# Three row-sum DMAs per item issued from ScalarE's queue instead of SyncE's, in a fused cross-attention and FFN kernel

## The reference, cut to what matters

```python
q, k, v = Wq @ ln(x), Wk @ ctx, Wv @ ctx
x1 = x + Wskip @ ln(x) + softmax(q.T @ k / sqrt(128)) applied to v   # 1024 x 256 scores
w  = (unpack_nibbles(qweight) - round(zeros / scales)) * scales        # 1024 x 1024
y  = x1 + ln(x1) @ w + bias
```

## Time and profile before

| | us |
|---|---|
| three runs | 566.91, 565.77, 566.85 (median 566.85) |
| the profiled execution | 567.06 |
| its span, first to last instruction | 565.2 |
| TensorE busy (matmuls) | 511.2 (90% of the span) |
| VectorE busy | 440.3 (78%) |
| GpSimd busy | 426.3 (75%) |
| ScalarE busy | 376.0 (67%) |

### The profile page before, as it was taken

One profiled execution on the slowest core, in us unless ns is written; L12 is line 12 of the kernel. 1 busy time (PEld: TensorE's weight loads), 2 busy tenths in 40 slices (PEclk: granted clock), 3 DMA queues, 4 the chain that ended last, 5 costly groups with the idle time before them and its releaser, 6 DMA issues.

```text
span 565.2 us, 9260 instructions
## 1 busy us (share of the span) xinstructions
PE 511.2 (90%) x2700; PEld 314.5 (56%) x2700; DVE 440.3 (78%) x1009; ACT 376.0 (67%) x844; POOL 426.3 (75%) x619
## 2 busy tenths in 40 slices
PE   2167789999999999999999999999999999999976
PEld 2054455656665665555566666555656665565532
DVE  2967778888988788888988878888898888886631
ACT  2277767776677677677677777767667776776510
POOL 1252778889888888888988888887988888888653
PEclk9996999999999999999999999999999999999989
DMA  8023678779778878888888988887888798866652
GB/s 316 29 66 66 130 160 184 175 174 191 172 165 160 169 180 187 183 176 182 168 185 164 163 175 182 178 189 169 184 172 174 177 146 183 195 122 147 139 118 92
DMA packets 236787, 91.65 MB, mean 162 GB/s; under 512 B 219200, under 2 KB 223808, under 8 KB 236736
## 3 DMA queue, kind: packets, MB, share of 16 engines
q1 hardware_dynamic: 236016, 90.92, 75.0%
q10 hardware_dynamic: 720, 0.14, 0.1%
HBM read 23.87 MB, written 16.78 MB: 72 GB/s over the span
## 4 chain that ended last, share of the span: by engine, by line
PE 48%; DVE 20%; SPq 10%; DMA 7%; ACT 6%; issue 5%; POOL 3%; POOLq 0%; ACTq 0%
PE ps_y L730 27%; PE ps_e L691 7%; DMA sb_xnt_lo<-sb_xn_lo 6%; PE ps_o L714 5%; SPq L173 4%; SPq L179 4%; PE ps_o L710 3%; SPq L165 3%; DVE sb_x L500 3%; DVE sb_st L434 3%; DVE sb_neg_max L481 2%; DVE sb_p_lo L490 2%; DVE sb_st L505 2%; ACT sb_p_hi L358 2%; PE ps_kv L699 2%
## 5 line engine op out<-in xcount | busy, mean ns | idle before, releaser
L730 PE MATMUL ps_y<-sb_wf,sb_xnt_hi 128*128 128x512 f16 x512 | 195.8, 382 | 13.7 <-DMA sb_xnt_lo<-sb_xn_lo 13.5
L730 PE MATMUL ps_y<-sb_wf,sb_xnt_lo 128*128 128x512 f16 x512 | 195.1, 381 | 0.0
L349 ACT ACTIVATE sb_prob<-ps_e,sb_neg_max 128x256 f32<-128x256 f32 x256 | 118.3, 471 | 62.5 <-DVE sb_neg_max L481 62.4
L235 POOL TENSOR_SCALAR sb_prob<-sb_prob,sb_rsum 128x256 f32<-128x256 f32 x256 | 122.1, 488 | 33.7 <-DVE sb_rsum L486 33.5
L490 DVE TENSOR_TENSOR sb_p_lo<-sb_prob,sb_p_hi 128x1024 f16<-128x1024 f32 x64 | 78.1, 1221 | 45.5 <-ACT sb_p_hi L358 45.5
L277 POOL TENSOR_TENSOR sb_xn_lo<-sb_xn,sb_xn_hi 128x512 f16<-128x512 f32 x64 | 76.1, 1208 | 45.4 <-ACT sb_xn_hi L376 45.4
L691 PE MATMUL ps_e<-sb_k_hi,sb_xc_hi 128*128 128x256 f32 x256 | 85.9, 336 | 22.3 <-DVE sb_v_lo L476 12.2
L730 PEld LDWEIGHTS ps_y<-sb_wf,sb_xnt_hi 128*128 128x128 f16 x512 | 50.2, 98 | 80.2 <-DMA sb_xnt_lo<-sb_xn_lo 17.7
L229 POOL TENSOR_TENSOR sb_o<-sb_prod,sb_x 128x512 f32<-128x512 f32 x64 | 80.7, 1280 | 8.9 <-DVE sb_prod L524 8.9
L481 DVE TENSOR_REDUCE sb_neg_max<-ps_e 128x2 f32<-128x512 f32 x128 | 84.9, 682 | 0.8 <-PE ps_e L691 0.2
L358 ACT ACTIVATE sb_p_hi<-sb_prob 128x1024 f16<-128x1024 f32 x64 | 67.3, 1051 | 22.3 <-issue 22.3
(11 more groups left out here) (96 smaller groups left out, 917.6 us busy)
## 6 DMA issues: line engine op xcount, KB each, us to landing
sb_x<-in_x_dram SPq DMA_DIRECT2D x32, 512.0 KB, 4.0
out_dram<-sb_o SPq DMA_DIRECT2D x64, 256.0 KB, 2.5
sb_ctx<-in_ctx_dram SPq DMA_DIRECT2D x32, 128.0 KB, 2.7
sb_q<-in_L_ffn_qweight_dram SPq DMA_DIRECT2D x4, 512.0 KB, 9.1
sb_seed_l<-sb_rs SPq DMA_DIRECT2D x96, 0.5 KB, 2.2
sb_pt_hi<-sb_p_hi SPq DMA_TRANSPOSE x64, 4.3
sb_pt_lo<-sb_p_lo SPq DMA_TRANSPOSE x64, 3.3
sb_scale_row<-in_L_ffn_scales_dram SPq DMA_DIRECT2D x1, 512.0 KB, 10.8
```

Of the source, the lines that this page charges most:

```text
L235: last = pool.tensor_scalar(prob[:, j, t, :], prob[:, j, t, :], rsum[:, j, t:t + 1], P_SCALE, ALU.mult, ALU.mult)
L349: done = act.activation(prob[:, j, t, :], ps_e[j % 2][:, t, :], ACT.Exp, bias=neg_max[:, j, t:t + 1], accum_out=esum[:, j, t:t + 1])
L730: pe.matmul(ps_y[h][:, :], xnt_p[s][:, par, kt, :], wf[:, kt, h * HALF:(h + 1) * HALF], start=kt == 0 and s == 0, stop=False)
```

## The change

The three row-sum DMAs leave turn_xn on SyncE, and a new turn_row_sum(a) on ScalarE issues them, right behind xn_high(a). ScalarE now waits for rs3 itself, and from the third item on for y_done[1] of two items earlier, since that FFN still reads the buffer of seed_l. Transfers, sizes, buffers and semaphores stay the same.

```diff
@@ turn_xn(a), on SyncE
                 sp.dma_start_transpose(xnt_hi[:, par, :, :],
                                        xn_hi[:, :, :].rearrange("c k r -> c (k r)")).then_inc(xnt_loaded[par], 16)
-                sp.wait_ge(rs3_done, a + 1)
-                if a == 0:
-                    sp.wait_ge(seed_made, 3)
-                for k, row in ((0, 0), (1, 1), (0, 32)):
-                    sp.dma_start(seed_l[row:row + 1, par, :].bitcast(F32),
-                                 rs3[:, par, k:k + 1].bitcast(F32)).then_inc(rs_loaded[par], 16)
                 sp.wait_ge(xnlo_done, a + 1)
@@ on ScalarE
+            def turn_row_sum(a):
+                par = a % 2
+                act.wait_ge(rs3_done, a + 1)
+                if ran(a, 2):
+                    act.wait_ge(y_done[1], a - 1)
+                if a == 0:
+                    act.wait_ge(seed_made, 3)
+                for k, row in ((0, 0), (1, 1), (0, 32)):
+                    act.dma_start(seed_l[row:row + 1, par, :].bitcast(F32),
+                                  rs3[:, par, k:k + 1].bitcast(F32)).then_inc(rs_loaded[par], 16)
@@ step(t), on ScalarE
                 if ran(a):
                     xn_high(a)
+                    turn_row_sum(a)
```

## The result

The changed kernel took 557.47 us (median of 6 runs, 555.77 to 558.77) against 566.88 for the kernel before (6 runs beside it): a ratio of 0.984, 95% interval 0.981 to 0.986. The forecast was 554.3, in a range from 551.0 to 572.0. One of the six runs of the kernel before took 679.29 us, the other five 565.77 to 567.09; the median is the same with it or without it to 0.1 us. The profiled execution took 558.77 us with a span of 557.0; that of before took 567.06. So 8.3 us went in the profiled executions, where the sum said 12.6, and 9.4 us by the medians.

What follows compares the result with a forecast made beforehand. The prediction took the late transpose xnt_lo, behind three small DMAs on SyncE, as lengthening about one step in three. Gains of 10.0 + 1.7 + 0.9 = 12.6 us took 567.06 to 554.5, by the median 554.3; range 551.0 to 572.0.

Steps and rivals of the forecast that it cites:

- What bounds the kernel: On SyncE, three small DMAs (1.89 us of issue) delay xnt_lo; TensorE waits 8.7 us in ten like steps.
- What the change removes: SyncE loses 1.89 us between xnt_hi and xnt_lo; gains 10.0 in like steps, 1.7 at the start, 0.9 at the end.
- I take 10.0, between them: Gain over 28 like steps, chosen between 8.7 us (TensorE's waits) and 11.2 us (a pace of 15.38).
- the prediction's other way to this term: Like-step gain taken from the waits themselves, 8.7 us; a pace of 15.47 would give 8.7 again.
- The start: Ahead of the first FFN, the same kind of wait for a transpose shrinks: 1.7 us gained, 1.89 at most.
- The end: At the last items, item 31's xn_lo on GpSimd then binds: 0.9 us gained, perhaps lost if the clock falls again.
- What the change adds: On ScalarE, waits and three DMAs behind xn_hi make the next centre 0.7 us later, covered by idle time.
- D: Time by which ScalarE's next centre is later: 0.7 us taken, 0 to 2.0 possible; gain gone at 1.74.
- Rival 1: ScalarE's DMAs wait until xn_hi (L376) ends: D = 2.0, step 16.04, 571.5 us, slower; chance 0.13.
- Rival 2: Small packets of a second queue delay the transposes, or D is near 1.6: about half the gain, 561 us; chance 0.12.
- Rival 3: SyncE's and ScalarE's queues take turns, so DMAs wait for transposes: D = 3.0, step 17.0, 598 us; chance 0.10.
- Rival 4: Nothing to be seen, by a D of 1.7 to 1.8 or other work replacing the wait: 566 us; chance 0.05.

Runs made afterwards that it cites:

- e2: The kernel before, with the three row-sum DMAs kept on SyncE but issued behind the transpose of xn_lo: 555.26 us, ratio 0.980.
- e1: The changed kernel with the row-sum DMAs issued for the first two items only, later items reusing those rows: 555.12 us, ratio 0.980.
- e4: The changed kernel with GpSimd's first output half moved into its 1.44 us gap ahead of xn_lo: 555.5 us, ratio 0.981.
- e8: The changed kernel with GpSimd's first output half moved into its gap ahead of xn_lo, except for the last item: 553.02 us, ratio 0.976.
- e10: The kernel before, row-sum DMAs on SyncE behind xn_lo's transpose, plus one spare activation on ScalarE where the change has its DMAs: 553.75 us, ratio 0.978.
- e3: The changed kernel with ScalarE waiting for the end of xn_hi before it issues the row-sum DMAs: 565.4 us, ratio 0.998.
- e11: The changed kernel run once more, unaltered, on the same chip: 557.24 us, ratio 0.984.
- e9: The kernel before, row-sum DMAs on SyncE behind xn_lo's transpose and GpSimd's first output half in its gap except for the last item: 552.37 us, 0.975.
- e6: The kernel before, its DMAs left on SyncE, with three more of the same size on ScalarE into a spare buffer: 567.64 us, ratio 1.002.
- e5: The kernel before, with GpSimd's first output half moved into its gap ahead of xn_lo: 574.48 us, ratio 1.015.
- e7: The changed kernel with three more small DMAs on ScalarE into a spare buffer, six in all: 591.42 us, ratio 1.044.

## Why the prediction was right, and where its sum was off

**What bounds the kernel.** Right. The three DMAs on SyncE stood on the path; e2, which only moves them behind xnt_lo, takes 11 us away.

**What the change removes.** The mechanism is right: xnt_lo is issued right behind xnt_hi and the wait fell from 8.7 to 0.3 us. The term of the like steps was mis-sized: 7.1 us in place of 10.0. The step that failed is "I take 10.0, between them", with the pace of 15.38 as one end. It took TensorE's own 15.38 for the next bound, and did not look at GpSimd. Behind the late transpose stood a second circuit, GpSimd's and ScalarE's, which at its best takes 15.47 us. e1 shows it in its chain, e4 and e8 by filling GpSimd's gap: the pace is then 15.41 and 15.39. Without that, 28 x 15.47 = 433.2 us was the floor (e1 433.1, e2 433.6, e10 433.1), 8.7 us under 441.9. That the waits of the earlier trace rows sum up to 8.7 as well, and that one of VectorE's intervals was 15.47, looks like a hit of the prediction's other way to this term, but it is not shown to be more than chance: in the kernel before no step of GpSimd was under 15.71 us. Why its circuit was longer there than after stays open; VectorE's slowed sb_wsk_lo (e3) is a candidate. The remaining 8.7 - 7.1 = 1.6 us go with the DMAs' new place: e11 took 1.9 us more than e10 in these steps, and more of GpSimd's 26 steps are long ones of 15.7 us and over (seven and eight with the change, five in e2, four in e1, two in e10). The prediction's sign that value_scale would come every 15.4 us was not met: the pace was 15.53.

**The start.** 1.7 forecast, 2.2 measured with the change. But e11, the same kernel, had its first FFN at 68.95, which would make it 3.9, over the 1.89 that the prediction took for the most; the other kernels' came between 68.7 and 71.5 us. So this term scatters by more than the miss. The clock has a part in it: in 60 to 72 us its mean was 0.73 in this profile and 1.00 in e11's. A window of the changed kernel, whose columns are the stretch, its length, busy us of PE, PEld, DVE, ACT and POOL, TensorE's granted clock, DMA share and GB/s:

```profile
60.00:72.00 12.00, 11.61 (x51) 7.74 (x52) 9.51 (x24) 10.46 (x23) 8.73 (x16) 0.73 0.79 136
```

**The end.** Forecast 0.9 us less, measured 1.1 more. The chain after, its last part, and the window behind it:

```profile
537.74 2.28 POOL sb_xn_lo L271 x2
540.04 3.06 DMA sb_xnt_lo<-sb_xn_lo
543.15 5.31 PE ps_y L736 x16
```

```profile
544.00:546.00 2.00, 2.00 (x7) 0.76 (x6) 0.00 (x0) 0.00 (x0) 0.00 (x0) 0.57 0.23 87
```

The prediction named the binding step, item 31's xn_lo on GpSimd, and it does bind: TensorE waited 2.33 us for its transpose. TensorE's timeline before, the first matmul of the last FFN, and the stretch of 4 us around it, with the columns given above:

```profile
553.12 0.39 PE L730 MATMUL ps_y<-sb_wf,sb_xnt_hi 128*128 128x512 f16 x1
```

```profile
550.00:554.00 4.00, 4.00 (x21) 1.77 (x19) 1.00 (x2) 0.00 (x0) 1.26 (x1) 1.00 0.54 131
```

From the 28th step's FFN to the last one it was 553.12 - 514.75 = 38.4 us, and is 543.15 - 505.39 = 37.8: 0.6 us gained of the 0.9. Then comes what the sum left out. Before, the slow half, 5.32 us at a clock near the lower level, was item 30's, and the last FFN, queued behind it without a wait, ran at a granted clock of 1.00. After, TensorE stood 2.33 us ahead of the last FFN, and this one's first half took 5.31 us, at a granted clock of 0.57 in 544 to 546 us. Nothing runs behind it that could cover that: about 5.3 - 3.6 = 1.7 us lost, and 0.6 - 1.7 = -1.1. The prediction had the fall of the clock as a bound, worth the 0.9 at most; it was worth twice that, because the slow stretch moved from the last FFN but one to the last.

The wait alone does not bring the fall. TensorE's timeline in e10, the same matmul, and a window behind it:

```profile
539.50 0.39 PE L736 MATMUL ps_y<-sb_wf,sb_xnt_hi 128*128 128x512 f16 x1 [2.24 <-DMA sb_xnt_lo<-sb_xn_lo]
```

```profile
541.00:543.00 2.00, 2.00 (x11) 0.97 (x9) 0.00 (x0) 0.00 (x0) 0.00 (x0) 1.00 0.53 204
```

The wait is as long, the clock stays at 1.00, and the first half takes 3.62 us. So it was in e1, e2 and e9. Among the profiles with small DMAs on ScalarE in every step, the clock fell in this half in six of seven (not in e6); among the others in one of six (e5). Whether the DMAs have a part in it is open.

**What the change adds.** Right, and close. The first DMA was issued ahead of xn_hi and the other two during it, where the prediction had all three ahead of it; D was 0.7 as forecast, and it came through nowhere (e10). Each DMA took 0.62 us in the median, against the 0.6 taken from SyncE. All 96 of them, by line: duration in ns, least, median and longest; first and last start.

```profile
L380 ACTq DMA_DIRECT2D sb_seed_l<-sb_rs x96: 476/624/851, 62.1 to 538.3; - x96
...
DMA to landing us min/median/max: 1.9/3.7/5.4
```

**Rival 1** did not occur in the change, since the sequencer runs ahead, but e3 and e7 show that it exists. Its formula was 0.4 us a step too dear at D = 2.1 (e3) and, at e7's 3.1, 17.1 against 16.48.

**Rival 2** occurred in small: not at the transpose of xn_lo, but as 1.1 to 1.9 us in all 28 like steps (434.8 and 435.0 us with the change, 433.1 to 433.6 in e1, e2 and e10; 1.4 by e6), with TensorE waiting for the low probabilities' transposes. The rest of the 2.2 us between the medians of e2 and the change, and of the 3 between e10 and e11, lies at the end in the profiles, where the clock fell in the one and not in the other. That the part in the like steps is the packets' follows only from leaving out the other suspect, ScalarE's lateness (e10). Nor is it shown how they would delay the transposes: the median landing (from the page and the view of DMAs) of pt_hi is 4.2 us with the change and 3.9 in e10, that of xnt_hi 3.6 and 3.3, that of pt_lo 3.2 and 3.3. My reading of the long transposes, that an instruction packet holds them up, was not tested either and stays open. The traces speak for it: of the 17 transposes before, 79 to 510 us, whose issue took over 1.9 us, 16 have a packet of the instruction queue within 0.5 us of their start. In the changed kernel an xnt_hi of 2.39 us is still there at 266.68.

**Rival 3** is refuted: the DMA of ScalarE at 247.93 took 0.48 us, and the two beside SyncE's transposes at 248.35 and 249.62 took 0.68 us each; the queues do not take turns of a transpose's 1.3 us. By the Trainium skill, Perfetto Trace Analysis, section DMA Instruction, HWDGE, the generator is locked by one sequencer at a time and the issue's time holds the wait. The issues here are no longer than SyncE's own, 1.89 / 3 = 0.63 us, so this trace does not agree: no such wait shows.

What does show is in the landing of the small DMAs, 3.7 us with the change against 2.2 in e10 (both from the page). Nobody waits for it.

**Rival 4** did not occur; the chances (0.72 faster) came from these cases and the time lay inside the range, 3.2 us over the forecast.

## What to carry to other kernels

When a wait is taken off the path, the gain is its size or the distance to the next circuit, whichever is less; so work out the period of every engine's circuit, GpSimd's with its answers from ScalarE too, not of the bounding engine alone. An engine 77% busy can be the bound: look at where it idles, and if these are answers to its own results, its circuit is closed. Moving small DMAs behind a critical transpose on the same queue did as much here as moving them to another engine, and was 2 us better by the medians, with intervals that overlap by a little.

## What the runs showed of the hardware

- ScalarE's sequencer issued a DMA 0.3 us ahead of the start of an activation that stands before it in the program (247.93 and 248.23), with another one running; a following activation waited for the issue to end.
- Three small DMAs on ScalarE beside SyncE's transposes are issued at the usual 0.62 us each but land 3.7 us after, against 2.2 behind the transposes; with them there the like steps took 1.1 to 1.9 us more in all (e1, e2, e10 against the change and e11).
- VectorE's 128x1024 fp32 to fp16 subtraction took 1.85 us instead of 1.21 when it began under an addition of GpSimd and ran into the next subtraction there, and GpSimd's pair of 128x512 subtractions 3.01 instead of 2.38; the addition, which had begun first, kept its 1.27 us (e4, e5).
- TensorE's granted clock was 0.57 in a 2 us stretch shortly behind a wait of 2.33 us, between its levels of 1.2 and 2.4 GHz and nearer the lower, and the sixteen matmuls there took 5.31 us instead of 3.63. Behind a wait of 2.24 us in e10 it stayed at 1.00.
